# Self attention: the row norm ahead of the projections moved from ScalarE to VectorE, the first norm left on ScalarE

## The chip, the cores and the metric

The kernel runs on one core of one Trainium2 chip. The metric is the device time of one execution in microseconds (us), the median of several runs. The engines are TensorE (PE in the rows; PEld is its weight load), VectorE (DVE), ScalarE (ACT), GpSimd (POOL) and SyncE (SP). All run in parallel, each through its own instructions in order, and wait for each other by semaphores.

## The reference

The program is a small decoder on x of 64 images x 128 rows x 128 channels: a state space model, self attention, cross attention, an MLP and further stages, each with a residual and a norm of the rows. The change is in self attention (`_mha(x, x, ...)` with `causal=True`; 16 heads of 32 channels). What matters of it:

```python
def _ln(x, g, b):
    m = jnp.mean(x, -1, keepdims=True)
    v = jnp.var(x, -1, keepdims=True)
    return (x - m) * jax.lax.rsqrt(v + 1e-05) * g + b
...
x = _ln(xx, ln1_g, ln1_b)                       # the first norm
x = x + _mha(x, x, a1_wq, ...)
...
xn = _ln(x, lnx_g, lnx_b)                       # the norm for the projections
q = jnp.einsum('bsc,hcd->bhsd', xn, wq)
a = jax.nn.softmax(jnp.einsum('bhsd,bhtd->bhst', q, k) * D ** (-0.5), axis=-1)
a = a * mask                                    # causal, after the softmax
o = jnp.einsum('bhst,bhtd->bhsd', a, v)
```

## The kernel before

`wide_attention_phase` (line 584) holds both wide attentions: the call at line 2859 is self attention (`own` is true), the one at 2863 cross attention. The 64 images are worked through in groups of GROUP = 4; there are 16 groups here. Each engine runs one loop over beats t = -1 to 68, one image per beat, as a software pipeline. In beat t TensorE makes the second scores of image t-2 (lines 806 to 821), the output projection of image t-4 (`project`, line 851), the sums of image t-3 (830), the first scores of image t+1 (794), the weighted values of image t-3 (844) and the turned maxima of image t (804). Into this it puts the 13 projection jobs of the next group: one of transposes (737, "x"), four q (741), four k (743), four v (745). The lists `late` and `early` say in which beat of a group each job runs.

The softmax takes two passes: first scores, whose negated row maxima VectorE forms (`maxima`, line 1044, four instructions per image), then second scores onto which the maxima are added on TensorE by small matmuls (line 816), and the exponential by ScalarE (line 911, two instructions per image). The second scores of an image go into banks from which the maxima of the image two ahead have to be read first: `second_scores` waits for `max_ready`, row group by row group. GpSimd multiplies the probabilities with the causal mask (`masked`, line 1173, four instructions of 128x512 per image).

The norms of a group run two groups ahead of its beats (`norms(t)` in each engine, g = t // 4 + 2, p = t % 4). First norm (x1): statistics by VectorE at p = 0 (lines 117 and 121), power -0.5 on GpSimd (126, 128) and there the shift -mean * rstd (`shifts`, 1109 and 1112), then at p = 1 ScalarE writes XC = X * rstd + shift (`x1_norm`, through `moved`, line 929), and GpSimd multiplies and adds the weights of the norm (1126, 1129). Second norm, for the projections: statistics of XC by VectorE at p = 2, power and shift by GpSimd at p = 2 (`in_inv`), and at p = 3 ScalarE writes xin (`in_norm`, `moved` again, line 929, four instructions of 128x128). TensorE transposes xin in the next beat (737). `pool_step` counts GpSimd's steps, POOL per group. In cross attention this second norm is done by VectorE's own `in_norm` through `normalise`, whose instruction (line 134) subtracts the mean and multiplies by rstd:

```python
op = dve.tensor_scalar(dst(b), src(b), mv[:, b, 0:1], rstd[:, b:b + 1], ALU.subtract, ALU.mult)
```

VectorE's order in a beat is: `split`, `add`, the early v jobs (987), `norms`, `maxima` of image t+1, `scaled` of image t-3 (1052), the late v jobs. ScalarE's is: exponentials, inverse of the sums, turned maxima, the emptying of q and k, `norms`. GpSimd's is: `masked` of image t-2, `advance` of image t-4 (1179), `norms`.

Of the kernel before, what the change touches and what calls it, by code (L numbers as in the profile page):

```python
# [24 lines left out]
P = 128  # L25
GROUP = 4
# [104 lines left out]
def normalise(dve, dst, src, mv, rstd):  # L131

    for b in range(GROUP):
        op = dve.tensor_scalar(dst(b), src(b), mv[:, b, 0:1], rstd[:, b:b + 1], ALU.subtract, ALU.mult)  # L134
    return op
# [448 lines left out]
def wide_attention_phase(nc, env, name, wd, w, kind):  # L584
# [4 lines left out]
    X, XB, XC, NG = env["X"], env["XB"], env["XC"], env["NG"]  # L589
    own = kind == "self"  # L590
# [7 lines left out]
    with Phase(nc, name) as ph:  # L598
# [8 lines left out]
        xin = ph.sb("xin", [P, GROUP, C])  # L607
# [5 lines left out]
        mv = ph.sb("mv", [P, 2, GROUP, 2])  # L613
        rstd = ph.sb("rstd", [P, 2, GROUP])
        power = ph.sb("power", [P, GROUP])
        shift = ph.sb("shift", [P, 2, GROUP])
        if own:
            pm = ph.sb("pm", [P, 2, 4, GT])
        else:
# [40 lines left out]
        N_DVE = sum(n for n, (*_, e) in zip(outs, jobs) if e == "dve")  # L660
        K_DVE = 0 if own else 1
        VEC = 4 * GROUP
        POOL = 9 if own else 4
        BEATS = range(-1, N + 5)

        def there(n):
# [210 lines left out]
        @block.scalar  # L877
        def _(act):
            act.preload_act_table_set("natural_log_exp_and_others")
            act.wait_ge(loaded, 16)  # L880

            def empty(g, n):
                what, i, e = jobs[n]
                if e != "act":
                    return
                act.wait_ge(proj_mm, g * NJ + n + 1)
                if what == "x":
                    op = act.activation(xT[:, :], pj[g * NJ % 2 if own else 0][:, :], ACT.Identity)
                elif what == "c":
                    op = act.activation(cT[:, :], pj[1][:, 0:2 * TK], ACT.Identity)  # L890
                elif what == "q":
                    if i == 0 and g >= 2:
                        act.wait_ge(s2_mm, (g - 1) * GROUP)
                    op = act.activation(qT[:, g % 2, i, :], pj[(g * NJ + n) % 2 if own else i % 2][:, :], ACT.Identity,
                                        bias=bias_q[:, i:i + 1], scale=SCALE)
                elif own:
                    op = act.activation(kT[:, g % 2, i, :], pj[(g * NJ + n) % 2][:, :], ACT.Identity, bias=bias_k[:, i:i + 1])
                else:
                    for j in range(NT - 1):
                        act.activation(kT[:, g % 2, j, :].rearrange("p (a h t) -> p h a t", a=2, h=2),  # L900
                                       pair[:, :, k_cols(j)].rearrange("p h (a t) -> p h a t", a=2), ACT.Identity,
                                       bias=bias_k[:, j:j + 1]).then_inc(by_act, 1)
                    return
                op.then_inc(by_act, 1)

            def probabilities(n):
                act.wait_ge(s2_mm, n + 1)
                if n >= 2:
                    act.wait_ge(pv_mm, n - 1)
                for i in range(2):  # L910
                    act.activation(pT[0:TK, n % 2, 2 * i:2 * i + 2, :], scores[i][0:TK, :, :], ACT.Exp).then_inc(exp_ready, 2)  # L911

            def inverse(n):
                act.wait_ge(sum_mm, n + 1)
                if n:
                    act.wait_ge(oT_ready, n)
                act.activation(rinv[:, :], sb[:, :], ACT.Ln).then_inc(ln_ready, 1)
                act.wait_ge(ln_ready, n + 1)
                act.activation(rinv[:, :], rinv[:, :], ACT.Exp, scale=-1.0).then_inc(rinv_ready, 1)

            def turned(n):
                act.wait_ge(turn_mm, n + 1)
                if n >= 2:
                    act.wait_ge(s2_mm, n - 1)
                act.activation(nmT[:, n % 2, :], sb[:, 0:T], ACT.Copy).then_inc(nmT_ready, 1)

            def moved(dst, src, k):
                for b in range(GROUP):
                    op = act.activation(dst(b), src(b), ACT.Identity, scale=rstd[:, k, b:b + 1], bias=shift[:, k, b:b + 1])
                return op  # L930

            def x1_norm(g):
                act.wait_ge(pool_step, g * POOL + 4)
                moved(lambda b: XC[:, g * GROUP + b, :], lambda b: X[:, g * GROUP + b, :], 0).then_inc(x1_normed, 1)

            def in_norm(g):
                act.wait_ge(pool_step, (g + 1) * POOL)
                if g:
                    act.wait_ge(proj_mm, (g - 1) * NJ + 1)
                moved(lambda b: xin[:, b, :], lambda b: XC[:, g * GROUP + b, :], 1).then_inc(xin_ready, 1)  # L940

            def norms(t):
                g, p = t // GROUP + 2, t % GROUP
                if own and g < NG:
                    if p == 1:
                        x1_norm(g)
                    if p == 3:
                        in_norm(g)

            if own:  # L950
                x1_norm(0)
                in_norm(0)
                x1_norm(1)
            for g, n in FRONT:
                if jobs[n][:2] == ("q", 0):
                    act.wait_ge(folded, FOLDED)
                empty(g, n)
            for t in BEATS:
                if there(t - 2):
                    probabilities(t - 2)  # L960
                if there(t - 3):
                    inverse(t - 3)
                if there(t):
                    turned(t)
                for g, n in late_jobs(t):
                    empty(g, n)
                norms(t)

        @block.vector
        def _(dve):  # L970
# [22 lines left out]
            def x1_stats(g):  # L993
                if g:
                    dve.wait_ge(pool_step, (g - 1) * POOL + 4)
                    dve.sem_inc(mark, 1)
                row_stats(dve, lambda b: X[:, g * GROUP + b, :], stats[:, 0], mv[:, 0], vec, g * VEC, mark)
# [14 lines left out]
            def in_norm(g):  # L1012
                dve.wait_ge(pool_step, (g + 1) * POOL)
                if g:
                    dve.wait_ge(proj_mm, (g - 1) * NJ + 1)
                normalise(dve, lambda b: xin[:, b, :], lambda b: XC[:, g * GROUP + b, :], mv[:, 0], rstd[:, 0])\
                    .then_inc(xin_ready, 1)
                normalise(dve, lambda b: ctx_t[0:TK, g % 2, b, :], lambda b: ctx_t[0:TK, g % 2, b, :],
                          mv[0:TK, 1], rstd[0:TK, 1]).then_inc(xin_ready, 1)

            def norms(t):
                g, p = t // GROUP + 2, t % GROUP
                if g < NG:
                    if own and p == 0:
                        x1_stats(g)
                    if p == 2:
                        in_stats(g)
                    if not own and p == 3:
                        in_norm(g)

            def split(n):
# [46 lines left out]
            dve.tensor_scalar(wv, wv, gy, None, ALU.mult).then_inc(folded, 1)  # L1078
            dve.wait_ge(folded, FOLDED)
            if own:  # L1080
                x1_stats(1)
            in_stats(1)
            for g, n in FRONT:
# [18 lines left out]
        def _(pool):  # L1102
# [4 lines left out]
            def shifts(k, base):  # L1107
                pool.wait_ge(pool_step, base)
                pool.tensor_tensor(shift[:, k], mv[:, k, :, 0], rstd[:, k], ALU.mult).then_inc(pool_step, 1)
                pool.wait_ge(pool_step, base + 1)  # L1110
                pool.sem_inc(mark, 1)
                pool.tensor_scalar(shift[:, k], shift[:, k], -1.0, None, ALU.mult).then_inc(pool_step, 1)
# [18 lines left out]
            def in_inv(g):  # L1131
                if own:
                    pool.wait_ge(vec, (g + 1) * VEC)
                    if g:
                        pool.wait_ge(xin_ready, g)
                    pool.sem_inc(mark, 1)
                    inv_std(pool, power[:, :], mv[:, 1], rstd[:, 1], pool_step, g * POOL + 5)
                    shifts(1, g * POOL + 7)
                else:
                    if g:  # L1140
                        pool.wait_ge(xin_ready, 2 * g)
                    pool.wait_ge(vec, g * VEC + 2 * GROUP)
                    pool.sem_inc(mark, 1)
                    inv_std(pool, power[:, :], mv[:, 0], rstd[:, 0], pool_step, g * POOL)
                    pool.wait_ge(vec, (g + 1) * VEC)
                    pool.sem_inc(mark, 1)
                    inv_std(pool, power[0:TK, :], mv[0:TK, 1], rstd[0:TK, 1], pool_step, g * POOL + 2)
# [1903 lines left out]
```

## Time and profile before

| | |
|---|---|
| median of 3 runs | 3683.49 us (3678.88 to 3685.28) |
| profiled execution | 3674.72 us |
| its span, first to last instruction | 3672.9 us |
| mean granted TensorE clock | 0.949 of full speed |
| busy, share of the span | PE 89%, PEld 58%, DVE 65%, ACT 54%, POOL 54% |

The page cuts the span into 40 equal slices of 91.8 us and gives the busy tenths of each engine in each:

```profile
PE   7999999996999999888999999969999799999376
...
DVE  5888888885555555575555548667777735555365
ACT  5666666663566665434555654336665445555254
POOL 5777877785777877671111116437777601103565
PEclk9999999998999999998999999979999979997698
```

Self attention lies in slices 10 to 16. The costliest instructions of the stage in the page's list are these (line, engine, operation, output<-input by name, shapes, count | busy us, mean ns | idle time of the engine just before, and its releaser):

```profile
L1173 POOL TENSOR_TENSOR self_pm<-self_pT,weights 128x512 f32<-128x512 f32 x256 | 322.3, 1296 | 58.3 <-ACT self_pT L911 56.9
L1044 DVE TENSOR_REDUCE self_nmax<-self_scores 128x4 f32<-128x512 f32 x256 | 158.5, 681 | 84.1 <-PE self_scores L794 84.1
L911 ACT ACTIVATE self_pT<-self_scores 128x1024 f32<-128x1024 f32 x128 | 123.7, 1018 | 77.3 <-PE self_scores L820 54.7
```

A timeline row gives the start in us of the span, the duration of the merged row, the engine, line, operation and operands, the number of instructions in it (x4 is four in a row), and in brackets the idle time of the engine before it with the releaser.

### The profile page before, as it was taken

Reading aid. Unit: us, or ns where it says so; the run is one execution under the profiler, and the core shown is the slowest. Engines: PE = TensorE matmul, PEld = TensorE weight load, DVE = VectorE, ACT = ScalarE, POOL = GpSimd, SP = SyncE. Lnnn points to the kernel's source line nnn. Section 1 sums busy time; section 2 is a strip of 40 time slices with the busy share of each in tenths; the row PEclk is TensorE's granted clock in tenths of the full one; section 3 lists DMA queues with packets and bytes.
Section 4 is the critical chain, followed back from the end, with each engine's and each line's share of the span. In section 5 each row is a group of like instructions: output and inputs, shape, how many; then the busy total and the mean of one; then the engine's idle time right before and its main releaser. Section 6 shows DMA issues by size and latency. Waiting matters only on the chain. (4 is left out here: it accounts for less than half of the span.)

```text
span 3672.9 us, 102246 instructions
## 1 busy us (share of the span) xinstructions
PE 3278.7 (89%) x41297; PEld 2120.4 (58%) x41297; DVE 2391.7 (65%) x5639; ACT 1983.8 (54%) x3570; POOL 1999.3 (54%) x1774
## 2 busy tenths in 40 slices
PE   7999999996999999888999999969999799999376
PEld 3554454443555555655666667645555567777375
DVE  5888888885555555575555548667777735555365
ACT  5666666663566665434555654336665445555254
POOL 5777877785777877671111116437777601103565
PEclk9999999998999999998999999979999979997698
DMA  4222222224700000000000000000000000000364
GB/s 145 91 84 86 87 86 84 86 84 162 244 2 2 2 2 2 15 3 12 5 5 5 4 6 1 8 7 2 2 2 2 9 17 18 6 6 17 106 171 115
DMA packets 50281, 164.67 MB, mean 45 GB/s; under 512 B 11822, under 2 KB 23217, under 8 KB 40784
## 3 DMA queue, kind: packets, MB, share of 16 engines
q1 hardware_dynamic: 45520, 150.43, 12.4%
q0 software_dynamic: 4352, 8.47, 0.7%
q8 instruction: 296, 4.85, 0.5%
q14 instruction: 113, 0.93, 0.1%
HBM read 149.89 MB, written 43.65 MB: 53 GB/s over the span
## 5 line engine op out<-in xcount | busy, mean ns | idle before, releaser
L496 DVE TENSOR_TENSOR_SCAN XC<-ssm_dA,ssm_db 128x2048 f32<-128x2048 f32 x128 | 565.4, 4418 | 108.1 <-PE ssm_db L352 95.5
L559 POOL TENSOR_TENSOR XC<-XC,XB 128x1536 f32<-128x1536 f32 x128 | 505.6, 3950 | 179.1 <-DVE XC L496 133.9
L366 PE MATMUL ssm_y<-XC,weights 128*128 128x512 f32 x1024 | 470.0, 602 | 2.5 <-POOL XC L559 2.3
L445 ACT ACTIVATE ssm_dA<-ssm_delta,ssm_nega 128x508 f32<-128x508 f32 x512 | 325.1, 707 | 83.6 <-DVE XC L496 83.1
L1173 POOL TENSOR_TENSOR self_pm<-self_pT,weights 128x512 f32<-128x512 f32 x256 | 322.3, 1296 | 58.3 <-ACT self_pT L911 56.9
L366 PEld LDWEIGHTS ssm_y<-XC,weights 128*128 128x128 f32 x1024 | 186.7, 190 | 214.2 <-issue 202.6
L1179 POOL TENSOR_TENSOR XC<-XC,XB 128x128 f32<-128x128 f32 x128 | 58.7, 459 | 399.4 <-DVE XB L1058 399.4
L2394 POOL TENSOR_TENSOR XC<-XC,weights 128x512 f32<-128x512 f32 x128 | 161.7, 1284 | 111.1 <-ACT XC L2230 111.1
L1044 DVE TENSOR_REDUCE self_nmax<-self_scores 128x4 f32<-128x512 f32 x256 | 158.5, 681 | 84.1 <-PE self_scores L794 84.1
L126 POOL TENSOR_SCALAR narrow_rstd<-narrow_mv 128x4 f32<-128x4 f32 x16 | 3.7, 229 | 377.6 <-DVE narrow_mv L121 377.6
L1510 DVE TENSOR_REDUCE narrow_nmax<-narrow_scores 128x4 f32<-128x308 f32 x256 | 105.0, 471 | 156.6 <-PE narrow_scores L1327 156.5
L352 PEld LDWEIGHTS ssm_db<-XB,ssm_dxT 32*128 32x128 f32 x4096 | 134.7, 187 | 98.3 <-DVE XC L496 64.1
L352 PE MATMUL ssm_db<-XB,ssm_dxT 32*128 32x128 f32 x4096 | 160.5, 285 | 24.6 <-DVE XC L496 23.1
L2402 POOL TENSOR_TENSOR XC<-XC,weights 128x512 f32<-128x512 f32 x128 | 161.3, 1282 | 34.1 <-ACT XC L2239 33.9
L1660 PEld LDWEIGHTS mlp_yp<-weights,mlp_h 128*128 128x128 f32 x1024 | 133.2, 192 | 58.1 <-issue 56.4
L911 ACT ACTIVATE self_pT<-self_scores 128x1024 f32<-128x1024 f32 x128 | 123.7, 1018 | 77.3 <-PE self_scores L820 54.7
L911 ACT ACTIVATE cross_pT<-cross_scores 77x1024 f32<-77x1024 f32 x128 | 123.6, 1015 | 72.9 <-PE cross_scores L820 59.6
L1435 ACT ACTIVATE narrow_pT<-narrow_scores 77x1024 f32<-77x1024 f32 x128 | 123.6, 1015 | 70.7 <-PE narrow_scores L1353 61.1
L1688 ACT ACTIVATE mlp_h<-mlp_hp,mlp_bias 128x512 f32<-128x512 f32 x128 | 88.0, 688 | 107.6 <-PE mlp_hp L1652 107.4
L1044 DVE TENSOR_REDUCE cross_nmax<-cross_scores 128x4 f32<-128x308 f32 x256 | 103.9, 466 | 57.5 <-PE cross_scores L794 57.5
L1652 PE MATMUL mlp_hp<-mlp_zT,weights 128*128 128x512 f32 x256 | 133.2, 607 | 1.5 <-ACT mlp_zT L1682 1.5
L1660 PE MATMUL mlp_yp<-weights,mlp_h 128*128 128x128 f32 x1024 | 134.2, 275 | 0.0
(430 smaller groups left out, 8270.9 us busy)
## 6 DMA issues: line engine op xcount, KB each, us to landing
XB<-c_rows SPq DMA_DIRECT2D x64, 1024.0 KB, 4.6
sorted<-in_padding SPq DMA_DIRECT2D x1, 33280.0 KB, 110.0
experts_we<-in_w_experts SPq DMA_DIRECT2D x72, 323.0 KB, 3.2
experts_rt<-sorted SPq DMA_DIRECT2D x72, 65.0 KB
ssm_xT<-in_xT SPq DMA_DIRECT2D x16, 256.0 KB, 4.6
XC<-in_w_experts SPq DMA_DIRECT2D x9, 256.0 KB, 3.3
weights<-in_w_self SPq DMA_DIRECT2D x1, 1412.0 KB, 7.5
cross_ctx_t<-in_ctx SPq DMA_DIRECT2D x16, 77.0 KB
```

The source lines that it names most:

```text
L352: mm = pe.matmul(of_batch(db, b)[:, :, 32 * c:32 * c + 32], dxT[rows, slot, half, c, :], diag(slot, c)[rows, nq, :].rearrange("p (k t) -> ...
L366: mm = pe.matmul(yp[half][:, :].rearrange("p (b t) -> p b t", b=GROUP), ident, of_state(states(32, at), k), start=(k == 0 and nq == 0 and ...
L445: o = act.activation(dA[:, p % 2, :].rearrange("p (b k t) -> p b k t", b=GROUP, k=4)[:, :, k, 1:T], by_batch(delta[:, slot, half, :])[:, : ...
L496: dve.tensor_tensor_scan(states(0, p).rearrange("p m t -> p (m t)"), dA[:, p % 2, :], db[:, :], 0.0, ALU.mult, ALU.add).then_inc(h_ready, 1)
L559: pool.tensor_tensor(states(32, p).rearrange("p (b k) t -> p b k t", k=4)[:, :, 0:3, :], states(0, p).rearrange("p (b k) t -> p b k t", k= ...
L911: act.activation(pT[0:TK, n % 2, 2 * i:2 * i + 2, :], scores[i][0:TK, :, :], ACT.Exp).then_inc(exp_ready, 2)
L1044: dve.tensor_reduce(nmax[:, r, :], sc[r][:, 0:4 * TK].rearrange("p (h t) -> p h t", h=4), AX.X, ALU.max, negate=True).then_inc(max_ready, 1)
L1173: pool.tensor_tensor(pm[:, n % 2, r, :].rearrange("p (h t) -> p h t", h=4), pT[:, n % 2, r, :].rearrange("p (h t) -> p h t", h=4), bcast(V ...
L1652: pe.matmul(hp[j][:, :], w2[:, j * P:(j + 1) * P], zT[:, g % 2, :]).then_inc(h_mm, 1)
L1660: mm = pe.matmul(yp[g % 2][:, b * C:(b + 1) * C], h[:, g % 2, j, b * T:(b + 1) * T], w3[:, j * C:(j + 1) * C], start=(j == 0), stop=(j == 3))
L2394: pool.tensor_tensor(a1(b, r), a1(b, r), bcast(tri, 1, 4), ALU.mult).then_inc(m1_pool, 1)
L2402: pool.tensor_tensor(a2(b, r), a2(b, r), bcast(tri0, 1, 4), ALU.mult).then_inc(m2_pool, 1)
```

## The change

For self attention alone, the second norm leaves ScalarE. ScalarE's `in_norm` is taken out, and VectorE's `in_norm`, until now for cross attention only, is called at p = 3 in both, ahead of `maxima`; for self attention it uses slot 1 of the statistics and returns after xin. GpSimd no longer forms the shift for this norm, so it has 7 steps per group in place of 9, and the shift tile shrinks to one slot. Group 0 is normalised by VectorE after the folding of the weights and ahead of the first-norm statistics of group 1. The first norm stays as it was.

```diff
--- before.py
+++ after.py
@@ -613,7 +613,7 @@
         mv = ph.sb("mv", [P, 2, GROUP, 2])
         rstd = ph.sb("rstd", [P, 2, GROUP])
         power = ph.sb("power", [P, GROUP])
-        shift = ph.sb("shift", [P, 2, GROUP])
+        shift = ph.sb("shift", [P, 1, GROUP])
         if own:
             pm = ph.sb("pm", [P, 2, 4, GT])
         else:
@@ -660,7 +660,7 @@
         N_DVE = sum(n for n, (*_, e) in zip(outs, jobs) if e == "dve")
         K_DVE = 0 if own else 1
         VEC = 4 * GROUP
-        POOL = 9 if own else 4
+        POOL = 7 if own else 4
         BEATS = range(-1, N + 5)
 
         def there(n):
@@ -933,23 +933,14 @@
                 act.wait_ge(pool_step, g * POOL + 4)
                 moved(lambda b: XC[:, g * GROUP + b, :], lambda b: X[:, g * GROUP + b, :], 0).then_inc(x1_normed, 1)
 
-            def in_norm(g):
-                act.wait_ge(pool_step, (g + 1) * POOL)
-                if g:
-                    act.wait_ge(proj_mm, (g - 1) * NJ + 1)
-                moved(lambda b: xin[:, b, :], lambda b: XC[:, g * GROUP + b, :], 1).then_inc(xin_ready, 1)
-
             def norms(t):
                 g, p = t // GROUP + 2, t % GROUP
                 if own and g < NG:
                     if p == 1:
                         x1_norm(g)
-                    if p == 3:
-                        in_norm(g)
 
             if own:
                 x1_norm(0)
-                in_norm(0)
                 x1_norm(1)
             for g, n in FRONT:
                 if jobs[n][:2] == ("q", 0):
@@ -1013,8 +1004,11 @@
                 dve.wait_ge(pool_step, (g + 1) * POOL)
                 if g:
                     dve.wait_ge(proj_mm, (g - 1) * NJ + 1)
-                normalise(dve, lambda b: xin[:, b, :], lambda b: XC[:, g * GROUP + b, :], mv[:, 0], rstd[:, 0])\
+                k = 1 if own else 0
+                normalise(dve, lambda b: xin[:, b, :], lambda b: XC[:, g * GROUP + b, :], mv[:, k], rstd[:, k])\
                     .then_inc(xin_ready, 1)
+                if own:
+                    return
                 normalise(dve, lambda b: ctx_t[0:TK, g % 2, b, :], lambda b: ctx_t[0:TK, g % 2, b, :],
                           mv[0:TK, 1], rstd[0:TK, 1]).then_inc(xin_ready, 1)
 
@@ -1025,7 +1019,7 @@
                         x1_stats(g)
                     if p == 2:
                         in_stats(g)
-                    if not own and p == 3:
+                    if p == 3:
                         in_norm(g)
 
             def split(n):
@@ -1078,6 +1072,7 @@
             dve.tensor_scalar(wv, wv, gy, None, ALU.mult).then_inc(folded, 1)
             dve.wait_ge(folded, FOLDED)
             if own:
+                in_norm(0)
                 x1_stats(1)
             in_stats(1)
             for g, n in FRONT:
@@ -1135,7 +1130,6 @@
                         pool.wait_ge(xin_ready, g)
                     pool.sem_inc(mark, 1)
                     inv_std(pool, power[:, :], mv[:, 1], rstd[:, 1], pool_step, g * POOL + 5)
-                    shifts(1, g * POOL + 7)
                 else:
                     if g:
                         pool.wait_ge(xin_ready, 2 * g)
```

## Rows read from the trace of the kernel before

**Rows 1.** Busy us of PE, PEld, DVE, ACT, POOL in two stretches; clock, DMA, GB/s.

```profile
1085.00:1234.00 149.00, 143.18 (x2246) 87.99 (x2243) 83.06 (x210) 92.21 (x152) 118.77 (x127) 1.00 0.01 2
1234.00:1383.00 149.00, 143.29 (x2212) 87.27 (x2215) 84.46 (x213) 92.63 (x153) 118.74 (x128) 1.00 0.01 2
```

**Rows 2.** Timeline of TensorE in group 9 of self attention.

```profile
1199.08 0.23 PE L816 MATMUL self_scores<-self_nmT,self_pick 32*128 32x128 bf16 x4
...
1200.52 1.16 PE L851 MATMUL self_out<-weights,self_oT 128*128 128x128 f32 x8
...
1208.18 0.23 PE L816 MATMUL self_scores<-self_nmT,self_pick 32*128 32x128 bf16 x1 [0.37 <-DVE self_nmax L1044]
...
1209.61 1.16 PE L851 MATMUL self_out<-weights,self_oT 128*128 128x128 f32 x8
```

**Rows 3.** Timeline of VectorE, the same stretch.

```profile
1193.94 0.29 DVE L1058 TENSOR_TENSOR XB<-self_out,XB 128x128 f32<-128x128 f32 x1 [1.88 <-PE self_out L851]
1196.33 2.48 DVE L1044 TENSOR_REDUCE self_nmax<-self_scores 128x4 f32<-128x512 f32 x4 [2.09 <-PE self_scores L794]
1198.73 0.68 DVE L1052 TENSOR_TENSOR self_oT<-self_out,self_rinv 128x512 f32<-128x512 f32 x1
...
1205.64 2.48 DVE L1044 TENSOR_REDUCE self_nmax<-self_scores 128x4 f32<-128x512 f32 x4 [0.21 <-PE self_scores L794]
```

**Rows 4.** Timeline of ScalarE, the same stretch.

```profile
1192.94 1.94 ACT L911 ACTIVATE self_pT<-self_scores 128x1024 f32<-128x1024 f32 x2 [0.84 <-PE self_scores L820]
...
1197.58 1.64 ACT L929 ACTIVATE self_xin<-XC,self_shift,self_rstd 128x128 f32<-128x128 f32 x4
1200.71 1.94 ACT L911 ACTIVATE self_pT<-self_scores 128x1024 f32<-128x1024 f32 x2 [1.49 <-issue]
```

**Rows 5.** Timeline of GpSimd, the same stretch.

```profile
1193.35 0.20 POOL L1109 TENSOR_TENSOR self_shift<-self_mv,self_rstd 128x4 f32<-128x4 f32 x1
...
1194.12 5.05 POOL L1173 TENSOR_TENSOR self_pm<-self_pT,weights 128x512 f32<-128x512 f32 x4
```

**Rows 6.** Timelines of VectorE and GpSimd in a later stage (gla), at two places.

```profile
2580.80 1.10 DVE L134 TENSOR_SCALAR X<-gla_y,gla_mv,gla_rstd 128x128 f32<-128x128 f32 x4
...
2901.25 5.10 DVE L134 TENSOR_SCALAR X<-gla_y,gla_mv,gla_rstd 128x128 f32<-128x128 f32 x4
2906.27 1.27 DVE L2331 TENSOR_TENSOR XC<-gla_scores,weights 128x512 f32<-128x512 f32 x2
...
2901.31 2.51 POOL L2402 TENSOR_TENSOR XC<-XC,weights 128x512 f32<-128x512 f32 x2
2903.78 2.49 POOL L2394 TENSOR_TENSOR XC<-XC,weights 128x512 f32<-128x512 f32 x2
```

**Rows 7.** Timelines of VectorE and GpSimd in the MLP.

```profile
1514.40 2.09 DVE L134 TENSOR_SCALAR mlp_z<-XB,mlp_mvx,mlp_rstdx 128x128 f32<-128x128 f32 x4 [1.61 <-POOL mlp_rstdx L128]
...
1514.34 1.29 POOL L1749 TENSOR_TENSOR mlp_resid<-XC,weights 128x512 f32<-128x512 f32 x1
```

**Rows 8.** Timelines of VectorE and ScalarE at the start of self attention.

```profile
890.46 0.87 DVE L117 BATCH_NORM_STATS2 self_stats<-X 128x6 f32<-128x128 f32 x4 [0.17 <-POOL self_shift L1109]
...
894.16 1.65 ACT L929 ACTIVATE XC<-X,self_shift,self_rstd 128x128 f32<-128x128 f32 x4 [1.71 <-POOL self_shift L1112]
895.72 0.57 ACT L888 ACTIVATE self_xT<-self_proj 128x512 f32<-128x512 f32 x1
```

**Rows 9.** Granted clock in two stretches (as Rows 1), and TensorE's timeline around them.

```profile
918.40:921.80 3.40, 3.40 (x32) 2.14 (x25) 2.03 (x4) 0.35 (x2) 0.00 (x0) 0.50 0.96 318
...
928.70:932.00 3.30, 3.29 (x35) 2.55 (x36) 1.93 (x10) 0.28 (x1) 3.30 (x3) 0.50 0.83 258
...
917.95 1.71 PE L794 MATMUL self_scores<-self_kT,self_qT 32*128 32x128 f32 x32 [2.74 <-DVE self_nmax L1044]
...
928.71 2.09 PE L794 MATMUL self_scores<-self_kT,self_qT 32*128 32x128 f32 x32 [2.68 <-ACT self_pT L911]
...
938.94 1.17 PE L794 MATMUL self_scores<-self_kT,self_qT 32*128 32x128 f32 x32 [1.22 <-ACT self_pT L911]
```

## The prediction

> **What bounds the kernel now.** I read the page's slices first, to find the stage that the change touches: self attention runs from 878 to 1500 us of the span, and nothing else is edited. Then I asked for the busy time by engine over some eight groups of it [rows 1]. The reader sees there that TensorE works 96% of the time at the full granted clock, that GpSimd comes next with 80%, and that VectorE (56%) and ScalarE (62%) have much spare time. A stage with TensorE at 96% can gain at most the few per cent that are missing, and it loses whatever makes TensorE wait. So the next views are timelines of one beat, engine by engine, around the place from which the work is taken and the place to which it goes. I use group 9 (beats 28 to 31 of the loop, near 1200 us); the thirteen other groups normalised inside the loop repeat it, shifted by 36.6 us each, with the same gaps within 0.15 us.
>
> In the beat with t % 4 = 3, TensorE finishes the v projections and begins the second scores at 1199.08 without any wait; the output projection follows 1.44 us later [rows 2]. The second scores need the row maxima of the image two ahead, since they overwrite that bank. VectorE makes the four maxima from 1196.33 to 1198.81, in time by 0.3 us [rows 3]. One beat later they are late: the last of four ends at 1205.64 + 2.48 = 1208.12, TensorE starts on it at 1208.18, and the output projection comes 1.43 us after that [rows 2, 3]. So here VectorE is covered by only 0.3 us, behind a VectorE idle gap of 2.09 us, and that gap is where the change puts its work.
>
> **The part that is taken away.** ScalarE loses four activations, 1.64 us together [rows 4]. Behind them ScalarE waits 1.49 us for the second scores before it can start the exponentials [rows 4]: the 1.64 us become more idle time, and TensorE sees nothing of them. Value: 0, and a gain is bounded by the 0.1 us of GpSimd below. GpSimd loses the product and the negation of the shift, from 1193.35 on, right ahead of the four mask products [rows 5]. The first of these also needs the first exponential, of a pair that started at 1192.94 and took 1.94 us, so its half is done near 1193.9 [rows 4]. The mask products, now at 1194.12, can start 0.1 us sooner and no more. The change of the count per group from 9 to 7 costs nothing: it renumbers waits.
>
> **The part that is added.** VectorE gets four subtract-and-multiply instructions of 128x128 in the same beat, behind the add that ends at 1193.94 + 0.29 = 1194.23 and ahead of the maxima [rows 3]. Its wait is for the power on GpSimd, which is over before 1193.35 [rows 5]; the wait for the transposes of the group before is long fulfilled. With GpSimd idle, four such instructions take 1.10 us [rows 6], the row at 2580.80. They would then end at 1195.33, inside the gap. At that price the change would cost nothing here.
>
> But GpSimd is not idle there: its four mask products run from 1194.12 to 1199.17 [rows 5]. The trace has a place with the same pattern. At 2901.25 VectorE starts four of these instructions while GpSimd runs 128x512 products back to back from 2901.31 to 2906.27. The four take 5.10 us in place of 1.10, and the next VectorE instruction starts at 2906.27, just when GpSimd's fourth product ends [rows 6]. Each VectorE instruction waited until a GpSimd product was over, and by then the next product had started, so the next one waited for that. Where GpSimd has only one such product, four of them take 2.09 us: one waits, three pass [rows 7]. The mask products have the form of those at 2901 and no gap between them (5.05 us for four). They decide the matter, and the plain price of 1.10 us does not apply.
>
> The Trainium skill (Advanced Engine Details and Errata, VectorE Performance Modes, Mode Summary) says that the second SBUF port of VectorE is shared with GpSimd, and that VectorE instructions in a two-port mode and GpSimd's instructions block each other; a float32 operation with a scalar between SBUF tiles is eligible for that mode. This speaks against the change. It does not say which of the two waits: if it were GpSimd, the sum would be zero. The trace agrees with the rule and adds that VectorE is the one that waits (5.10 us against 1.10, with GpSimd's pace unchanged) [rows 6].
>
> So the sum for one group. The maxima start at 1199.17 in place of 1196.33 and end at 1199.17 + 2.48 = 1201.65. TensorE starts the last of its first four small matmuls 0.06 us later, at 1201.71, and the output projection 1.43 us after it, at 1203.14. Now it is at 1200.52: 2.62 us late. The product with the inverse sums (0.68 us behind the maxima, [rows 3]) is ready at 1202.3, ahead of that, so it adds nothing. The other three engines wait for TensorE from there on and shift with it, and the stall one beat later stays as it is. I take 2.6 us, between 2.5 (GpSimd's 0.1 given back) and 2.65. Groups 2 to 15 are normalised inside the loop beside mask products, 14 of them: 14 x 2.6 = **36.4 us**. Group 1 is normalised before any mask product exists, in a gap of several us: 0.
>
> At the start, group 0 is normalised by VectorE ahead of the statistics of group 1. They start now at 890.46 and move back by the 1.1 us. ScalarE's first norm of group 1 (894.16) hangs on them, and the emptying of the first transposes (895.72), for which TensorE waits, stands behind it in ScalarE's order [rows 8]. That gives **+1.0 us**, bounds -1.1 (the row norm itself is ready sooner, if only that counted) and +1.2.
>
> **The clock.** TensorE has two stretches with 2.7 us of idle time in the start of this stage. After each, the granted clock fell to 0.50 (1.2 in place of 2.4 GHz) for about 3.4 us, and the first scores behind the second took 2.09 us in place of 1.17; after a gap of 1.22 us it did not fall [rows 9]. The new stall has 2.6 us too, with three small matmuls in it. At half clock 3.4 us of work lose 1.7 us; I take 1.6, since a part may fall in the stall one beat later. How many of the 14 stalls bring such a fall no row says: 0 to 14, so 0 to 24 us. The length is that of the two gaps that did it, the small matmuls speak against. I take 8 of 14: 8 x 1.6 = **12.8 us**.
>
> Sum: 36.4 + 1.0 + 12.8 = 50.2 us. The profiled execution took 3674.7 us, its span 3672.9; the median of the runs is 3683.5, 0.2% above. The sum is of waits in absolute time, so I add it to the median: 3683.5 + 50.2 = **3733.7 us**, +1.4%.
>
> **The rivals.** (a) The stall without the clock: 37.4 us, 3720.9; with a fall in all 14, 36.4 + 1.0 + 23.8 = 61.2, 3744.7. Both are the ends of the forecast's own case, 3719 to 3746. (b) Two norms pass at each hand-over of the port, or the norm holds it once it has it. For it: at one product only one norm waited [rows 7]. Against: at 2901 each of four waited [rows 6]. In the first form the second mask product's end (about 1196.6) and a pair behind it put the maxima at 1197.1, 0.8 us late against a cover of 0.3: 0.5 x 14 + 1 = 8 us, 3691.5. In the second the norms end near 1196.3 and cost only the start: 3684.5. (c) Not slower: GpSimd is the one that yields. This holds if the four norms pass within the 2.09 us of the gap [rows 3]. They end at 1195.3, the mask products at most 1.1 us later, and their reader, the weighted sums one beat on, stands far behind. Then what remains is the start (+1.0 to -1.1) and GpSimd's 14 x 0.1 = 1.4 us: 3681.0 to 3684.5. Against it stand all five rows at 2901 and 2581 [rows 6]. A gain beyond 0.2% would need exponentials that wait for ScalarE in this beat; with 0.6 us each, 14 x 0.6 = 8 us, 3675. The 1.49 us of idle time ahead of them speak against it [rows 4]. (d) The norms hold up GpSimd as well as VectorE, each hand-over adding a norm (0.28 us) to the mask products: four of them, 1.1 us more per group, 15 us, 3749. Against: four products take 4.96 us at 2901, no longer than the 5.05 here [rows 5, 6].
>
> **How the numbers follow.** Forecast with its clock cases 0.80; (b) 0.07, half in each form; (c) 0.08, 0.03 of it in its faster form; (d) 0.05. A measurement of this kernel can tell 0.2% (7.4 us) from no change. Faster: 0.03. Same: 0.05 of (c) and the second form of (b), and with some doubt the first, 0.09. Slower: 0.88. The range for 8 in 10 is the forecast's case with a little room above for (d) and below for stalls that are partly covered: 3708 to 3749 us.
>
> **What the changed profile would show.** The four norms in the beat with t % 4 = 3 take about 5 us as a group, each near 1.3 us, against 1.3 us in all if I am wrong. The maxima behind them start when the fourth mask product ends. The small matmuls of the second scores get a wait for the maxima of about 2.6 us per group, while the period grows from 36.6 to 39.2 us or more. The granted clock in the stage falls below 1.00 in stretches of about 3.4 us. ScalarE's idle time before the exponentials grows by the 1.64 us. The prediction is wrong if the norms take 1.1 to 2.1 us, and its size is wrong if the clock stays at 1.00 or drops after every stall.

## The result, and the profile after

The changed kernel takes 3732.9 us (median of 4 runs, 3729.4 to 3739.3), the kernel before 3681.2 us (4 runs, the three of the table above among them): a ratio of 1.0135, with an interval of 1.0119 to 1.0151. It is 1.4% slower, against 3733.7 us forecast, within 3708 to 3749. The profiled execution took 3730.8 us, its span 3728.9.

The page of the changed kernel shows in its busy time, as totals, only that the norms moved:

```profile
span 3728.9 us, 102199 instructions
PE 3309.2 (89%) x41297; PEld 2140.5 (57%) x41297; DVE 2456.2 (66%) x5703; ACT 1958.0 (53%) x3506; POOL 1991.5 (53%) x1742
```

VectorE has 64 instructions and 64.5 us more, ScalarE 64 fewer and 25.8 us less. The 64 norms of one ScalarE activation each (0.48 us) would be 0.34 us each on a VectorE that nothing holds up, 22 us in all; so the 64.5 us already say that they are held up. The rows of the tile written by the norm give the time of one (ns, minimum, median, maximum):

```profile
L134 DVE TENSOR_SCALAR self_xin<-XC,self_mv,self_rstd x64: 335/1331/1340, 893.2 to 1469.9; 128x128 f32<-128x128 f32 x64
```

The median is four times the minimum. Where that happens is seen in the timelines of VectorE, GpSimd, TensorE and ScalarE, one group of the changed kernel near 1225 us (the line numbers of VectorE and GpSimd are five to nine smaller than before: L1038 is `maxima`, L1052 `add`, L1167 `masked`):

```profile
1222.60 0.29 DVE L1052 TENSOR_TENSOR XB<-self_out,XB 128x128 f32<-128x128 f32 x1 [1.88 <-PE self_out L851]
1222.81 5.07 DVE L134 TENSOR_SCALAR self_xin<-XC,self_mv,self_rstd 128x128 f32<-128x128 f32 x4
1227.80 2.47 DVE L1038 TENSOR_REDUCE self_nmax<-self_scores 128x4 f32<-128x512 f32 x4
...
1222.77 5.02 POOL L1167 TENSOR_TENSOR self_pm<-self_pT,weights 128x512 f32<-128x512 f32 x4 [0.83 <-ACT self_pT L911]
...
1228.62 0.21 PE L816 MATMUL self_scores<-self_nmT,self_pick 32*128 32x128 bf16 x1 [0.82 <-DVE self_nmax L1038]
1229.13 0.23 PE L816 MATMUL self_scores<-self_nmT,self_pick 32*128 32x128 bf16 x1 [0.30 <-DVE self_nmax L1038]
1229.72 0.22 PE L816 MATMUL self_scores<-self_nmT,self_pick 32*128 32x128 bf16 x1 [0.37 <-DVE self_nmax L1038]
1230.32 0.23 PE L816 MATMUL self_scores<-self_nmT,self_pick 32*128 32x128 bf16 x1 [0.37 <-DVE self_nmax L1038]
...
1231.75 2.07 PE L851 MATMUL self_out<-weights,self_oT 128*128 128x128 f32 x8
...
1231.94 1.94 ACT L911 ACTIVATE self_pT<-self_scores 128x1024 f32<-128x1024 f32 x2 [5.60 <-PE self_scores L820]
```

These are the answers to [rows 2 to 5]. The four norms fill 5.07 us in place of ScalarE's 1.64, from the add to the end of the mask products (1222.77 + 5.02 = 1227.79), and the maxima begin at 1227.80. TensorE, which had all four row groups at once at 1199.08, now gets them one by one, 0.6 us apart; it is idle for 0.82 + 0.30 + 0.37 + 0.37 = 1.86 us of the stall. ScalarE's wait ahead of the exponentials has grown by 4.1 us, from 1.49 to 5.60: about the 1.64 us of the relief, which became idle time, and the stall.

The output projection of this group took 2.07 us in place of 1.16. That is the clock. The busy time and granted clock in four stretches (PEclk is the number behind the bracket of POOL) show it at half behind the stall, and at full until the next:

```profile
1190.80:1194.10 3.30, 3.30 (x18) 2.56 (x15) 1.02 (x4) 1.94 (x2) 1.62 (x2) 0.50 0.00 0
1194.20:1231.60 37.40, 34.11 (x535) 20.34 (x534) 24.27 (x53) 19.23 (x31) 26.79 (x28) 1.00 0.01 2
1231.80:1235.00 3.20, 3.20 (x14) 2.49 (x11) 0.81 (x4) 1.94 (x2) 1.89 (x2) 0.50 0.00 0
1358.00:1433.00 75.00, 68.35 (x1038) 40.75 (x1037) 48.25 (x107) 40.40 (x64) 54.70 (x57) 1.00 0.01 2
```

The last row holds a stall (near 1393 us) without a fall. The starts of the groups' transposes tell what each part costs, as differences from group to group. The first two rows are of the kernel before, the others of the changed kernel:

```profile
1206.51 0.61 PE L737 MATMUL self_proj<-weights,self_xin 128*128 128x128 f32 x4
1243.09 0.61 PE L737 MATMUL self_proj<-weights,self_xin 128*128 128x128 f32 x4
...
1198.57 0.60 PE L737 MATMUL self_proj<-weights,self_xin 128*128 128x128 f32 x4
1239.36 0.61 PE L737 MATMUL self_proj<-weights,self_xin 128*128 128x128 f32 x4
...
1361.90 0.61 PE L737 MATMUL self_proj<-weights,self_xin 128*128 128x128 f32 x4
1401.11 0.61 PE L737 MATMUL self_proj<-weights,self_xin 128*128 128x128 f32 x4
```

A group with a fall takes 40.79 us, the one without 39.21. Before it was 36.58 (from 1206.51 to 1243.09). So the stall is 39.21 - 36.58 = 2.63 us and the fall 1.58 us.

Fourteen groups are normalised inside the loop, but not each of them has such a stall. VectorE, GpSimd and TensorE of the changed kernel in groups 2 and 3:

```profile
939.33 1.12 DVE L134 TENSOR_SCALAR self_xin<-XC,self_mv,self_rstd 128x128 f32<-128x128 f32 x4 [1.25 <-POOL self_rstd L128]
...
942.39 5.02 POOL L1167 TENSOR_TENSOR self_pm<-self_pT,weights 128x512 f32<-128x512 f32 x4 [3.10 <-ACT self_pT L911]
...
983.49 0.71 PE L794 MATMUL self_scores<-self_kT,self_qT 32*128 32x128 f32 x10 [2.03 <-issue]
```

The norms of group 2 come in a pause of GpSimd: the four take 1.12 us and are over before the mask products begin, so nothing is late. In group 3 they take 5.08 us, but TensorE itself had stood still for 2.03 us in that beat, for no reason that the profile shows, and did not have to wait for the maxima. The other 12 groups have the full stall. The clock fell behind 11 of these 12.

### The profile page after: what moved, and what is told of

The parts are those of the page before. It is cut to its first block and busy times, and to the rows that moved or that the text cites. A ratio compares the mean times of both kernels' runs of the same rounds, so it can differ in the third digit from the quotient of the medians.

```text
span 3728.9 us, 102199 instructions
## 1 busy us (share of the span) xinstructions
PE 3309.2 (89%) x41297; PEld 2140.5 (57%) x41297; DVE 2456.2 (66%) x5703; ACT 1958.0 (53%) x3506; POOL 1991.5 (53%) x1742
## 5 line engine op out<-in xcount | busy, mean ns | idle before, releaser
L1167 POOL TENSOR_TENSOR self_pm<-self_pT,weights 128x512 f32<-128x512 f32 x256 | 322.3, 1298 | 123.5 <-ACT self_pT L911 123.5
L1038 DVE TENSOR_REDUCE self_nmax<-self_scores 128x4 f32<-128x512 f32 x256 | 158.3, 679 | 51.8 <-PE self_scores L794 51.8
L2396 POOL TENSOR_TENSOR XC<-XC,weights 128x512 f32<-128x512 f32 x128 | 161.3, 1281 | 34.2 <-ACT XC L2233 33.9
L1038 DVE TENSOR_REDUCE cross_nmax<-cross_scores 128x4 f32<-128x308 f32 x256 | 103.9, 466 | 56.9 <-PE cross_scores L794 56.9
```

Source lines behind the costliest of these rows:

```text
L1038: dve.tensor_reduce(nmax[:, r, :], sc[r][:, 0:4 * TK].rearrange("p (h t) -> p h t", h=4), AX.X, ALU.max, negate=True).then_inc(max_ready, 1)
L1167: pool.tensor_tensor(pm[:, n % 2, r, :].rearrange("p (h t) -> p h t", h=4), pT[:, n % 2, r, :].rearrange("p (h t) -> p h t", h=4), bcast(V ...
L2396: pool.tensor_tensor(a2(b, r), a2(b, r), bcast(tri0, 1, 4), ALU.mult).then_inc(m2_pool, 1)
```

## The experiments

The kernels of one set were timed beside the kernel before on the same chip: 3682.6 us for the first set (the form, the place, three of four, the relief), 3699.9 us for the second (the addition, the half as long products, the order of ScalarE). Ratios are to that. The expectations of the second set were written for a kernel before of about 3682 us, so with them it is differences that can be compared, not times. "Period" is the time from group to group past 1010 us, read as above.

**The form of the instruction.** The norm is written with rstd as a second tensor input in place of a scalar.

```diff
-                normalise(dve, lambda b: xin[:, b, :], lambda b: XC[:, g * GROUP + b, :], mv[:, k], rstd[:, k])\
...
+                    for b in range(GROUP):
+                        op = dve.scalar_tensor_tensor(xin[:, b, :], XC[:, g * GROUP + b, :], mv[:, 1, b, 0:1],
+                                                      bcast(rstd[:, 1, b], 1, C), ALU.subtract, ALU.mult)
+                    op.then_inc(xin_ready, 1)
...
```

> The changed kernel, but the four norms of self attention are written as scalar_tensor_tensor (subtract the mean as a scalar, multiply by rstd broadcast along the row as a second SBUF input) in place of tensor_scalar, in the same place. Theory (the form waits): only the single-input form with scalars between SBUF tiles waits for GpSimd's products, since the 128x512 tensor_tensor of VectorE with two SBUF inputs ran in 0.69 us beside a GpSimd product of 3.96 us in the kernel before. Then the four take 1.3 to 1.5 us, the maxima start on time, the granted clock stays at 1.00 in the stage, and the time is that of the kernel before plus 0 to 2 us, 3681 to 3686. Rival 1 (place and length: four more instructions on VectorE behind the add are too much there, whatever their form): 3715 to 3735. Rival 2 (two SBUF inputs also wait for GpSimd): 3730 or more, the norms at 5 us for four.

Measured: 3739.3 us, 1.0152 (1.0128 to 1.0177), period 41.0 us. The timelines of VectorE and GpSimd in this kernel:

```profile
1224.12 5.31 DVE L1009 SCALAR_TENSOR_TENSOR self_xin<-XC,self_mv,self_rstd 128x128 f32<-128x128 f32 x4
...
1224.08 5.21 POOL L1170 TENSOR_TENSOR self_pm<-self_pT,weights 128x512 f32<-128x512 f32 x4 [0.92 <-ACT self_pT L911]
```

My own expectation fell, and the second rival held. The VectorE product of 0.69 us that I had taken for proof began at 304.91, 0.04 us ahead of GpSimd's at 304.95: it did not have to wait because it came first. The same VectorE line at 71.25 us came while a GpSimd product of 128x512 was running; there it took 0.87 us in place of 0.69. This form with two SBUF inputs waits just as the one with scalars. The Trainium skill (GPSIMD Engine Reference, Key points) names both: GpSimd shares its SBUF interfaces with VectorE, with contention for VectorE's instructions "in a 2-port perf mode or with two SBUF inputs". The trace agrees, at 5.31 us for four. The statistics, with one SBUF input, go by freely: one of self attention takes 0.28 us in the middle of a mask product of the kernel before as it does without one.

**The place in the queue.** The norms of the loop stand behind the maxima and the late v jobs.

```diff
-                    if p == 3:
+                    if not own and p == 3:
                         in_norm(g)
...
                 for g, n in late_jobs(t):
                     empty(g, n)
+                if own and t % GROUP == 3 and t // GROUP + 2 < NG:
+                    in_norm(t // GROUP + 2)
```

> The changed kernel with the norms of groups 1 to 15 called at the end of VectorE's beat, behind the maxima, the scaling and the late v jobs, in place of ahead of the maxima. By then GpSimd's mask products are over and one residual add of 1.27 us is left. Theory (what costs is that the norms are spread over the mask products ahead of the maxima): the four take 1.1 to 2.0 us, VectorE's idle gaps of the next beat (0.66 + 0.57 us and two of 0.2) hold most of it, the maxima of the next beat move by 0 to 0.5 us: 3682 to 3692. Rival (any place in this queue costs, because VectorE with these waits is the bound): 3710 or more.

Measured: 3687.0 us, within the theory's range, 1.0012 (0.9998 to 1.0026), period 36.58 us, clock 1.00 from 1050 to 1350 us. VectorE and GpSimd:

```profile
1208.89 2.48 DVE L1038 TENSOR_REDUCE self_nmax<-self_scores 128x4 f32<-128x512 f32 x4 [2.09 <-PE self_scores L794]
...
1213.09 1.13 DVE L134 TENSOR_SCALAR self_xin<-XC,self_mv,self_rstd 128x128 f32<-128x128 f32 x4
...
1206.68 5.05 POOL L1169 TENSOR_TENSOR self_pm<-self_pT,weights 128x512 f32<-128x512 f32 x4 [0.85 <-ACT self_pT L911]
```

The same four instructions on the same engine, still 5 us ahead of their reader, take 1.13 us and cost nothing per group. The period is that of the kernel before to the hundredth. VectorE had the room; the change used the wrong part of it. (The period excludes what the start of the stage costs.)

**Three of four.** The fourth norm goes behind the late v jobs, three stay ahead of the maxima. (`in_norm` takes the norms to make as its second argument; that part of the edit is left out.)

```diff
-                        in_norm(g)
+                        in_norm(g, range(3) if g > 1 else range(4))
...
+                if own and t % GROUP == 3 and 1 < t // GROUP + 2 < NG:
+                    in_norm(t // GROUP + 2, (3,))
```

> The changed kernel with three of the four norms ahead of the maxima and the fourth behind the late v jobs (groups 2 to 15). Theory (one mask product per norm): the maxima start when the third mask product ends, 1.25 us earlier than in the changed kernel, so the stall is 2.6 - 1.25 = 1.35 us per group, 19 us for 14, and plus 1 at the start. Of the clock: if it is the length of the stall that brings the fall to half, it stays at 1.00 with 1.35 us, and the time is 3681 + 20 = 3701; if any stall of this kind does, 11 x 1.6 = 18 us more, 3719. Rival (the group of four waits as a whole, not one by one): 3730.

Measured: 3702.7 us against 3701, 1.0050 (1.0031 to 1.0069), period 37.95 us: a stall of 1.37 us. The clock stayed at 1.00 from 1050 to 1350 us.

```profile
1218.59 3.84 DVE L1009 TENSOR_SCALAR self_xin<-XC,self_mv,self_rstd 128x128 f32<-128x128 f32 x3
1222.35 2.47 DVE L1042 TENSOR_REDUCE self_nmax<-self_scores 128x4 f32<-128x512 f32 x4
...
1226.54 0.33 DVE L1009 TENSOR_SCALAR self_xin<-XC,self_mv,self_rstd 128x128 f32<-128x128 f32 x1
```

Three take 3.84 us, the fourth, beyond the mask products, 0.33. One norm costs one mask product, and half the stall brings no fall of the clock: none of the 12 stalls past 1010 us was followed by one. So the clock's part is a term of its own. The shorter stall also has less idle time in it (two gaps of 0.37 us in place of 1.86 us in all); which of the two keeps the clock up isn't separated.

**Each half of the change alone.** First the relief: the kernel before without ScalarE's norm in groups 2 to 15. Then the addition: the kernel before with VectorE's norms added, into a tile of their own.

```diff
-                moved(lambda b: xin[:, b, :], lambda b: XC[:, g * GROUP + b, :], 1).then_inc(xin_ready, 1)
+                if g < 2:
+                    moved(lambda b: xin[:, b, :], lambda b: XC[:, g * GROUP + b, :], 1).then_inc(xin_ready, 1)
+                else:
+                    act.sem_inc(xin_ready, 1)
```

> The kernel before with ScalarE's norm for the projections left out for groups 2 to 15 (the projections of those groups then read the rows of group 1); all waits are kept. It measures what taking the norm off ScalarE is worth by itself. Theory: ScalarE waits for TensorE behind it, worth 0: 3679 to 3684. Rival (ScalarE's queue matters, and the loss of the change is a larger loss less a gain here): 3675 or less.

```diff
...
+                    if own and p == 3 and g > 1:
+                        dve.wait_ge(pool_step, (g + 1) * POOL)
+                        normalise(dve, lambda b: extra[:, b, :], lambda b: XC[:, g * GROUP + b, :], mv[:, 1], rstd[:, 1])
```

> The kernel before with everything kept, ScalarE's norm too, and the four tensor_scalar norms of groups 2 to 15 made by VectorE once more into a tile that nobody reads, ahead of the maxima, where the change has them. It is the added part alone. Theory: the norms wait for the mask products one by one (5.1 us for four), the stall is 2.6 us per group and the clock falls behind about 11 of 14: 36 + 18 = 54 us, 3725 to 3740, and the loss of the change is all in this part. Rival (part of the change's loss comes from the removed shift, the new waits or the later start of group 0): 3715 or less.

Measured: the relief 3684.6 us, 1.0004 (0.9990 to 1.0018), period 36.59 us; the addition 3752.1 us, 1.0139 (1.0120 to 1.0159), 52 us above the kernel before of its set where 54 were expected, period 40.8 us. The rows of the extra tile are those of the norm in the changed kernel:

```profile
L134 DVE TENSOR_SCALAR self_extra<-XC,self_mv,self_rstd x56: 340/1327/1344, 938.5 to 1477.4; 128x128 f32<-128x128 f32 x56
```

The minimum is that of group 2, which lies ahead of the mask products here too. The whole loss (1.0135) is in the addition, within the intervals, and the relief is worth nothing that shows. In this trace and in that of the two-input form all 12 stalls past 1010 us were followed by a fall of the clock.

**Half as long mask products.** Each is split into two of 128x256, and TensorE's wait for them counts eight per image in place of four; everything else is the changed kernel.

```diff
+                    for h in range(2):
+                        half_of = slice(2 * T * h, 2 * T * h + 2 * T)
+                        pool.tensor_tensor(pm[:, n % 2, r, half_of].rearrange("p (h t) -> p h t", h=2),
+                                           pT[:, n % 2, r, half_of].rearrange("p (h t) -> p h t", h=2),
+                                           bcast(V("mask"), 1, 2), ALU.mult).then_inc(mask_ready, 1)
```

> The changed kernel with each mask product of 128x512 split into two of 128x256 (self attention only). Theory (a norm waits for the one GpSimd instruction that runs when it comes, whatever its length): the four norms take 4 x 0.65 = 2.6 us, the maxima start 0.5 us late against a cover of 0.3, the stall is 0.2 to 0.5 us per group, no fall of the clock: 3685 to 3692. Rival (the norms get through only when GpSimd has no more work queued): they take 5 us as before, 3730 or more. Second rival (the split products cost GpSimd so much more that masks come late): the weighted sums wait for them, and GpSimd is busy over 90%.

```profile
1201.14 2.87 DVE L134 TENSOR_SCALAR self_xin<-XC,self_mv,self_rstd 128x128 f32<-128x128 f32 x4
1203.93 2.47 DVE L1038 TENSOR_REDUCE self_nmax<-self_scores 128x4 f32<-128x512 f32 x4
...
1201.10 5.56 POOL L1169 TENSOR_TENSOR self_pm<-self_pT,weights 128x256 f32<-128x256 f32 x8 [0.35 <-ACT self_pT L911]
...
1206.46 0.23 PE L816 MATMUL self_scores<-self_nmT,self_pick 32*128 32x128 bf16 x1 [0.16 <-DVE self_nmax L1038]
```

The norms are done after four of the eight pieces: 2.87 us, while GpSimd goes on to 1206.66. The period is 36.97 us, a stall of 0.39, and the clock stays at 1.00 from 1050 to 1350 us. So a norm waits for the one GpSimd instruction that is running when its turn comes, not for GpSimd's queue. GpSimd is busy 83% from 1050 to 1350 us, and no wait of TensorE for masks shows, so the second rival falls too. The expected time was missed: 3714.8 us, 1.0049 (1.0031 to 1.0066), is 15 us (by the medians) to 18 us (by the ratio) above the kernel before, where 3 to 10 were expected and 13 x 0.39 = 5.1 us and the start are accounted for. Its runs spread from 3699 to 3724 us, and the profiled one is the fastest; what the others lost isn't known.

**A better order for ScalarE.** In the kernel before TensorE waits 0.60 us per group for exponentials that stand behind ScalarE's first norm. That norm is moved ahead of the turned maxima, once beside the norms behind the maxima, and once in the kernel before.

```diff
                 if there(t - 3):
                     inverse(t - 3)
+                norms(t)
                 if there(t):
                     turned(t)
                 for g, n in late_jobs(t):
                     empty(g, n)
-                norms(t)
```

(In the kernel before `x1_norm` alone is moved so.)

> The kernel with the norms behind the maxima, and besides ScalarE's first norm in the beat with t % 4 = 1 moved from the end of its beat to ahead of the turned maxima, where ScalarE had 1.08 us idle. In the kernel before this norm held up the next exponentials, and TensorE waited 0.60 us for them in each group. Expected by the theory: 14 x 0.5 = 7 us below the kernel with the norms behind the maxima alone (3687), so 3680, 0.1% below the kernel before. Rival (the turned maxima or the emptying of q, now 0.1 to 0.6 us later, take it back): 3687.

> The kernel before with only ScalarE's first norm moved ahead of the turned maxima (both norms stay with ScalarE). Theory: the period of a group falls from 36.58 to about 36.0 us, 14 x 0.5 = 7 us: 3675. If it equals the kernel before, the 0.60 us wait for the exponentials is paid elsewhere. Compared with the same move beside VectorE's norm it says whether the norm on VectorE is worth anything once ScalarE is at a limit.

Measured: 3696.0 us, 0.9990 (0.9976 to 1.0004), and 3692.2 us, 0.9980 (0.9966 to 0.9995). Both have a period of 36.02 us, and TensorE's wait for the exponentials is gone from it. The second is 0.2% faster than the kernel before, 7.7 us by the medians, near 14 x 0.56 = 7.8; the interval reaches from 2 to 13 us. The first is 3.9 us faster by the medians, and its interval includes no change at all; that it beats the norms behind the maxima alone was not measured side by side and shows only in the period. VectorE's norm adds nothing to the period: with ScalarE's queue put right, taking more from it is still worth nothing.

**The kernel before and the changed kernel once more.** Most traces have TensorE idle at the start of the stage for no reason that the profile shows: 0 us in all in the kernel before, 0.2 with the half as long products, and 2.2 to 7.4 in the other eight of the nine changed programs (the expectation below counts five).

> The kernel before, unchanged, for a second trace. In the traces of five of the nine changed programs TensorE stands still in the first 110 us of self attention for 2 to 8 us in all, for nothing that the profile shows, while the DMA engines are fully busy; the trace of the kernel before had none of it. If that belongs to the moment and not to a program, this trace may show some too, with the same period of 36.58 us from 1010 us on. If it shows none again, the stalls may belong to the changed programs, and part of the change's loss with them.

> The changed kernel, unchanged, for a second trace. Its stall per group should be 2.62 us in all 14 groups, a group with a fall of the clock 40.8 us and one without 39.2, as in the first trace, with 9 to 14 falls, as the start of the stage lies otherwise against the rest. The unnamed stalls before 1010 us may come out otherwise than the 2.2 us of the first trace.

Measured: 3699.0 and 3749.6 us, one execution each; an execution of the kernel before beside them took 3708.9, so single times are loose by 10 us here and the traces have to tell. The kernel before shows such a stall too this time, 0.57 us ahead of one matmul of the weighted values and 0.93 at 981 us, and its second and third period are 2.0 and 1.6 us longer than in the first trace:

```profile
944.19 0.30 PE L845 MATMUL self_out<-self_pm,self_v 128*32 128x128 f32 x1 [0.57 <-issue]
```

From 1010 us on its period is 36.59 again. The changed kernel has 39.2 and 40.8 us again, and again 11 falls, here behind 13 stalls, since group 3 has one too: TensorE's stillness without a cause is only 0.3 us this time. In both traces the fall comes later behind the stall from group to group, from 2.2 us behind the first late small matmul up to 3.5; the next stall has none, and behind the one after it the fall comes at 1.9 us. So something beside the stall itself decides too. From its first matmul to its last add the stage took 622.1 and 676.7 us in the first pair of traces, 625.2 and 677.1 in the second: 54.6 and 51.9 us more.

## Why the prediction was right

**What bounds the stage**: right. TensorE kept its 96% only as long as nothing made it wait, and the relief of ScalarE was worth 0 (1.0004). The 1.49 us of idle time behind the norm told that from one row [rows 4].

**The price of four norms**: right, and this step decided the case. By the plain price of 1.10 us the change would have been free. The row at 2901.25 [rows 6] gave 5.10, the change had 5.07, and the maxima started at the end of the mask products. The experiments show the reason in three ways: a fourth norm beyond the mask products takes 0.33 us, norms behind the maxima take 1.13, and with pieces of half the length they take 2.87. My note that it must be the form of the instruction, in the first experiment, was wrong: I had generalised from one row in which VectorE came first.

**The stall**: the size was right, the count was not. Forecast were 2.6 us in 14 groups, 36.4 us. Measured were 2.62 to 2.63 in 12 groups of the first trace, 31.6 us, and in 13 of the second, 34.2. The prediction had said that the other groups repeat group 9 with the same gaps. Group 2 does not: in the kernel before VectorE is idle for 5.31 us ahead of its maxima in place of 2.09 [rows 3], and the norms found GpSimd at rest there. The distance from VectorE to TensorE was right: from the end of the maxima (1227.80 + 2.47 = 1230.27) to the output projection (1231.75) it is 1.48 us, against 0.06 + 1.43.

**The start**: forecast +1.0 us; from the load of the activation table to the first emptying of transposes ScalarE took 18.2 us in place of 17.3, +0.9. The norm itself was ready 1.0 us earlier and it did not matter, as the chain through the statistics of group 1 had said [rows 8].

**The clock**: a fall of the clock was right, the count was mis-sized. I took 8 falls of 1.6 us, 12.8; there were 11 of 1.58, 17.4. The size of one fall came from half of the 3.4 us in [rows 9] and held. The count was a choice between 0 and 14. Why it is 11 of 12 and 11 of 13 here, and 12 of 12 in two of the experiments, isn't shown.

**The sum**: with what was measured, the three terms are 31.6 + 17.4 + 0.9 = 49.9 us in the first pair of traces and 34.2 + 17.4 + 0.9 = 52.5 in the second, against 50.2 forecast. The stage took 54.6 and 51.9 us more. The idle time without a cause gives 2.2 us to the first difference and takes 1.2 from the second. In the first pair the changed kernel also had half clock from 931 to 938 us, where the first trace of the kernel before had it from 928.7 to 932.1 only; by half of the 3.4 us more that is an estimate of 1.7 us, and the second pair has the longer one in both kernels. That leaves 0.8 and 0.6 us unnamed. The medians differ by 51.8 us, and the ratio with its interval stands for 44 to 56.

So the close agreement of 3733.7 with 3732.9 is partly luck: one or two stalls too many (2 to 5 us) stood against three falls too few (4.6 us).

**The rivals**: (b) two norms per hand-over and (c) GpSimd yields were excluded by one row each, the tile's median of 1331 ns and the maxima's start. (d) GpSimd held up as well did not happen with the changed kernel (5.02 us for four products against 5.05), but it does a little with two tensor inputs (5.21). One thing in the chances is not as worded: 0.09 for the same time is (c) without its faster form and the second form of (b), 0.05 + 0.035; the first form of (b) was counted as slower.

## What to carry to other kernels

Before an elementwise operation is moved to VectorE, look at what GpSimd does in the very microseconds where it would land. If it streams long products there, one VectorE instruction of the two forms tried here (with scalars between SBUF tiles, or with a second SBUF input) costs the rest of a GpSimd instruction, here 1.3 us in place of 0.34; the busy shares of the two engines tell nothing of it. The same work some 5 us later was free per group, so move it within the queue before giving it up. And price relief by the wait behind the removed work: where an engine waits for the bounding engine anyway, taking work off it is worth nothing.

## What was unexpected in the hardware

A VectorE instruction with two SBUF inputs waits for GpSimd as well (5.31 us for four), though a row of the kernel before seemed to say otherwise, and GpSimd's own products go on almost as if nothing had happened: four take 5.02 us in place of 5.05 beside the form with scalars, 5.21 beside the other. The wait is for a single GpSimd instruction: cutting the products in two cut the norms from 5.07 to 2.87 us. A stall of 2.6 us on TensorE, with three small matmuls in it and 1.9 us of idle time, was followed by a fall of its clock to half in 11 of 12 and 11 of 13 cases in the two traces of the changed kernel and in all 24 (stalls of 2.6 and 2.8 us) of two experiments; a fall cost 1.58 us more, while none of 12 stalls of 1.37 us was followed by one. And at the start of the stage, while 33 MB are written by DMA, TensorE can stand still for 0 to 7.4 us in all with no cause that the profile shows; it happens with the unchanged kernel too. What it waits for stays open.
